# Second attention's stages begin with unit 4 of the second experts, and its values are divided by the softmax sums

## What is computed

```python
h = (x - mu) / jnp.sqrt(var + LN_EPS) * norm_w + norm_b
q, k, v = split(h @ qkv_w.T + qkv_b)                 # each L x C
w = jax.nn.softmax(jnp.einsum('ncq,nck->nqk', q, k * scale), axis=2)   # C x C
a = jnp.einsum('nqk,nck->ncq', w, v)
s = a @ proj_w.T + proj_b + x
# experts: every token is put in a slot of its two experts, 40 slots for each expert and row
y = relu(buf @ W1 + b1) @ W2 + b2;  f = sum over the two picks of p * y[slot]
x = x + s * silu(f)
```

## Time and profile before

| | |
|---|---|
| time, median of 3 runs | 1442.65 us (1442.06 to 1442.7) |
| profiled execution, its time | 1442.93 us |
| its span in the profile | 1441.2 us |
| busy: PE, DVE, ACT, POOL | 93%, 70%, 61%, 59% of the span |
| granted TensorE clock, mean | 0.988 of full speed |

### The profile page before, as it was taken

One profiled execution on the slowest core, in us unless ns is written; L12 is line 12 of the kernel. 1 busy time (PEld: TensorE's weight loads), 2 busy tenths in 40 slices (PEclk: granted clock), 3 DMA queues, 4 the chain that ended last, 5 costly groups with the idle time before them and its releaser, 6 DMA issues.

```text
span 1441.2 us, 32467 instructions
## 1 busy us (share of the span) xinstructions
PE 1344.9 (93%) x10039; PEld 1187.9 (82%) x10039; DVE 1007.4 (70%) x3163; ACT 879.5 (61%) x2257; POOL 845.3 (59%) x1675
## 2 busy tenths in 40 slices
PE   5999998998999999999999999999999999899964
PEld 4548897887899899899889988998998899788842
DVE  7817774666778677677768767776877777545765
ACT  3546775445677677677667667776767777522321
POOL 6257884443776665756656575565557576633462
PEclk9999999999999999999999999999999999999997
DMA  7017002423300000000000000000000000012231
GB/s 256 8 59 240 24 25 83 126 82 93 108 20 4 18 16 9 18 12 9 9 14 17 8 18 13 9 7 16 16 9 11 20 11 5 20 51 77 62 86 40
DMA packets 70203, 62.26 MB, mean 43 GB/s; under 512 B 10904, under 2 KB 58115, under 8 KB 70034
## 3 DMA queue, kind: packets, MB, share of 16 engines
q1 hardware_dynamic: 61842, 44.96, 10.3%
q0 software_dynamic: 8192, 15.23, 3.7%
HBM read 32.88 MB, written 25.17 MB: 40 GB/s over the span
## 4 chain that ended last, share of the span: by engine, by line
PE 79%; DVE 8%; issue 5%; POOL 4%; ACT 2%; DMA 1%; DVEq 1%; POOLq 0%; SPq 0%
PE sa L1895 17%; PE sc L1873 15%; PE mb L1902 13%; PE tr L1884 9%; PE sc L1732 4%; PE sc L1832 3%; PE mb L2113 2%; PE sc L1875 2%; DVE kept L1413 2%; PE sa L1737 1%; PE tr L1737 1%; POOL attn L799 1%; PE sc L2101 1%; POOL x_slots L770 1%; PE sc L1854 1%
## 5 line engine op out<-in xcount | busy, mean ns | idle before, releaser
L799 POOL TENSOR_SCALAR attn<-kept,rden 128x128 f32<-128x128 f32 (+3 forms) x512 | 289.4, 565 | 324.2 <-DVE rden L1417 299.1
L1406 DVE MAX8 top<-sc 128x8 f32<-128x144 f32 (+3 forms) x512 | 263.2, 514 | 221.4 <-PE sc L1875 219.4
L1873 PE MATMUL sc<-k_hl,x_hl 128*128 128x272 f32 (+3 forms) x1920 | 371.4, 313 | 3.2 <-DVE k_hl L1398 1.7
L1895 PE MATMUL sa<-wv,attnT 128*128 128x128 f32 x2560 | 370.8, 276 | 0.0
L1032 ACT ACTIVATE attnT<-tr 128x128 f32<-128x128 f32 (+3 forms) x512 | 223.2, 436 | 227.0 <-PE tr L1884 225.1
L1895 PEld LDWEIGHTS sa<-wv,attnT 128*128 128x128 f32 x2560 | 326.3, 192 | 2.0 <-issue 1.8
L1873 PEld LDWEIGHTS sc<-k_hl,x_hl 128*128 128x128 f32 x1920 | 282.0, 190 | 23.2 <-issue 13.0
L1026 ACT ACTIVATE ex<-sc,nmax 128x144 f32<-128x144 f32 (+3 forms) x512 | 276.9, 541 | 16.7
L1413 DVE SCALAR_TENSOR_TENSOR kept<-sc,top,ex 128x144 f32<-128x144 f32 (+3 forms) x512 | 284.3, 555 | 2.5 <-ACT ex L1026 0.8
L1884 PE MATMUL tr<-ident,attn 128*128 128x128 f32 x1280 | 229.5, 277 | 25.5 <-POOL attn L799 23.6
L1884 PEld LDWEIGHTS tr<-ident,attn 128*128 128x128 f32 x1280 | 138.9, 142 | 35.8 <-POOL attn L799 31.4
(11 more groups left out here) (334 smaller groups left out, 1935.8 us busy)
## 6 DMA issues: line engine op xcount, KB each, us to landing
x_slots<-sg SPq DMA_DIRECT2D x1, 4608.0 KB, 17.1
y_slots<-wv SPq DMA_DIRECT2D x18, 256.0 KB, 2.3
x_slots<-sg SPq DMA_DIRECT2D x1, 2560.0 KB, 16.5
y_pick<-x_slots SPq DMA_DIRECT2D x10, 256.0 KB, 2.8
fb<-L_ffn_b SPq DMA_DIRECT2D x2, 1024.0 KB
attn<-x_slots SPq DMA_DIRECT2D x8, 256.0 KB, 3.3
arena<-L_attn_x SPq DMA_DIRECT2D x8, 256.0 KB, 3.3
fb<-L_ffn_W SPq DMA_DIRECT2D x8, 256.0 KB, 6.3
```

Source lines behind the costliest of these rows:

```text
L799: pool.tensor_scalar(dst, src[:, NM:NM + P * (t + 1)], rden[:, t:t + 1], 1.0, ALU.mult, ALU.mult).then_inc(attn_ready.sem, 1)
L1406: dve.max(top8[:, t, :], src).then_inc(top_done.sem, 1)
L1873: pe.matmul(dst[:, lo:hi], x_hl[:, a, t * P:(t + 1) * P], k_hl[:, m, k, lo:hi], start=(i == 0), stop=(i == 2 and hi < w), skip_group_check ...
L1895: ins = pe.matmul(sa[:, t * C:(t + 1) * C], src[:, j * P:(j + 1) * P], wv[:, j, k, :], start=False, stop=False, skip_group_check=True)
```

## The change

The constant `C_FROM` = 4 takes the place of `E1` = 8: four slots go with each unit from unit 4 on, so slots 0 to 47 lie in units 4 to 15 and slots 48 to 69 in the tail. The slots behind which `take_z` and `gate` stand are renumbered. Units, slots and their matmuls are the same in number and shape. The second part: `weights` no longer multiplies the 128x128 weights by the reciprocal sums; ACT does it in the copy of the applied values (L1188), by a scale per partition, and PE turns the weights as soon as the exponentials are there. PE waits once more, at unit 4, for a read of bank `sa` (`sa_read`), and each `hnorm(r)` waits for its own row's kept input.

```diff
-        TAKE_Z = {16: 0, 24: 1, 32: 2, 36: 3, 44: 4, 52: 5, 60: 6, SLOTS_C: 7}
-        GATES = {18: 0, 26: 1, 34: 2, 38: 3, 46: 4, 54: 5, 62: 6, SLOTS_C + 1: 7}
+        TAKE_Z = {34: 0, 40: 1, 46: 2, 50: 3, 56: 4, 62: 5, 67: 6, SLOTS_C: 7}
+        GATES = {36: 0, 42: 1, 48: 2, 52: 3, 58: 4, 64: 5, 69: 6, SLOTS_C + 1: 7}
+        C_FROM = 4
...
                 if name == "apply":
                     act.wait_ge(aT_ps.sem, r + 1)
-                    act.activation(aT[r % 2], c_bank(i), ACT.Copy).then_inc(aT_ready.sem, 1)
+                    act.wait_ge(csum_ready.sem, r + 1)
+                    act.activation(aT[r % 2], c_bank(i), ACT.Copy, scale=csum[:, r % 2:r % 2 + 1]).then_inc(aT_ready.sem, 1)
...
             for n in range(UNITS_E):
-                slot = 4 * (n - E1)
+                slot = 4 * (n - C_FROM)
...
-                if n >= E1:
+                if n >= C_FROM:
                     evacuate_c(slot)
...
-            for i in range(4 * E1, SLOTS_C):
+            for i in range(4 * (UNITS_E - C_FROM), SLOTS_C):
                 evacuate_c(i)
...
             def hnorm(r):
                 dve.wait_ge(rstd1_ready.sem, rstd1_ready.at(r, 1))
+                dve.wait_ge(xn1_kept.sem, xn1_kept.at(r, 16))
...
-                dve.reciprocal(csum[:, r % 2:r % 2 + 1], csum[:, r % 2:r % 2 + 1])
-                dve.drain()
-                dve.tensor_scalar(cw[:, r % 2, :], cw[:, r % 2, :], csum[:, r % 2:r % 2 + 1], None, ALU.mult
-                                  ).then_inc(cw_ready.sem, 1)
+                dve.reciprocal(csum[:, r % 2:r % 2 + 1], csum[:, r % 2:r % 2 + 1]).then_inc(csum_ready.sem, 1)
...
-                if n == E1 - 1:
-                    dve.wait_ge(xn1_kept.sem, xn1_kept.at(B, 0))
+                if n == C_FROM - 1:
                     hnorm(0)
...
                 if name == "cwT":
-                    pe.wait_ge(cw_ready.sem, r + 1)
+                    pe.wait_ge(cexp_done.sem, r + 1)
...
+                if n == C_FROM:
+                    pe.wait_ge(sa_read.sem, sa_read.at(B - 1, 1))
```

More of the change, by code:

```diff
@@ L413, in build @@
         cexp_done = sig0("cexp_done")
-        cw_ready = sig0("cw_ready")
+        csum_ready = sig0("csum_ready")
         cwT_ps = sig0("cwT_ps")
```

## The result

The changed kernel takes **1438.33 us**, median of 11 runs (1437.14 to 1441.98); the kernel before took 1442.7 us beside it (11 runs, 1441.32 to 1444.17). The ratio is 0.997, with a 95% interval of 0.9961 to 0.9979. A second set of 5 runs took 1436.55 us, ratio 0.9957 (0.9944 to 0.9971). So it is faster by 0.2 to 0.6%, and the predicted 1438.7 us lies inside the first set of runs and 2.15 above the median of the second.

A forecast was written before the change was run, and what follows sets the result against it. The tail's serial slot chain bounds the kernel before, the gathers the changed one. Of 27.7 us off the tail, 10.8 come back in units and 12.9 go to gathers: 4.0 gained, 1442.65 to 1438.7 us, range 1435.3 to 1441.7.

The forecast's parts named there:

- Parts 1, 4 and 5: Units: two rows in, unit 14 10.27 us later; tail: slots wait on gathers, DVE free 5.7 us; end: span 4.0 shorter.
- the wait for block 8: At unit 8: PE's wait for the block's load goes, taking 1.33 us off the added cost of two rows.
- Part 2: Before unit 15's last relu: `take_z(2)` delays `down(15, 0)` and the gathers by 0.57 us, bounds 0 and 1.3.
- Part 3: POOL's 32 gathers of rows 4 to 7: first at 1385.83, 41.31 us to last start, row 7's data at 1429.7.
- the floor of 38.75: POOL's gathers of rows 4 to 7: 31 steps at 1.25 us throughout, in place of 41.31.
- Part 6: Sums divided later: only 0.3 us gained ahead of the gathers; about 1 us for each last row if gathers didn't bind.
- Gathers stretch: Rival, POOL's gathers: many more at the slow pitch, 0.50 us each, up to 12.9 more, 1451.6 us; chance 0.07.
- Units cost more: Rival, units 4 to 15: slots cost 0.25 us more a unit, 3 us lost, 1441.7 us; chance 0.08.
- Much faster: Rival, the end: gathers don't bind, the slot chain ends the kernel 16.8 us earlier, 1425.8 us; chance 0.03.

The follow-up runs named there:

- half_gathers: The changed kernel with 4 in place of 8 gathers for each of rows 4 to 7; 1424.15 us, ratio 0.9877.
- take2_late: The changed kernel with `take_z(2)` and gate 2 moved behind unit 15, from in front of its last relu; 1438.69 us, ratio 0.997.
- units_only: The changed kernel with weights still scaled by DVE and `cwT` waiting for them, so only the slots moved; 1437.29 us, ratio 0.9965.
- light_gates: The changed kernel with the gates of rows 3 to 6 replaced by one operation on one column; 1436.63 us, ratio 0.9961.
- after_again: The changed kernel measured once more with no edit; 1436.55 us, ratio 0.9957.
- sums_only: The kernel before (slots from unit 8) with only the later division by the sums, on values instead of weights; 1440.14 us, ratio 0.9985.
- from7: The changed kernel with slots beginning at unit 7 instead of 4, `take_z` and gates renumbered to suit; 1434.15 us, ratio 0.9944.

## Why the prediction was right, point by point

| step of the prediction | forecast | measured |
|---|---|---|
| unit 14 after unit 4 | 81.77 | 1362.42 - 1280.62 = 81.80 |
| unit 14 to `down(15, 0)` | 16.65 + 0.57 = 17.22 | 17.12 |
| first gather of row 4 after unit 4 | 105.51 | 105.51 |
| 32 gathers, first to last start | 41.31 | 40.29 |
| last gather to its data | 2.6 | 2.70 |
| DVE's wait for row 7 | 5.7 | 5.57 |
| row 7's `take_z` to the end | 7.45 | 7.48 |
| from unit 4 to the end | 156.88 | 155.98 |

**Parts 1, 4 and 5, the path and its new bound, were right.** Two rows cost what rows cost in units, the wait for block 8 went, and the end moved from the slots to the gathers. That the gathers bind is shown by half_gathers, and the 10.8 us that come back in the units by the first gather, 10.84 later than before from unit 4 on. The slots' chain runs at the gathers' pace as forecast: `take_z(4)`, `(5)` and `(6)` start at 1397.79, 1408.27 and 1418.44, each behind a wait for its gathers, where about 1398, 1408 and 1418.9 were given.

**Part 2, `take_z(2)`, was right in its sum and in its two terms.** The forecast was about 0.87 for the `take_z` and 0.3 back from the scaling, net 0.57. From unit 14 to `down(15, 0)` it took 16.65 us before, 17.12 in the changed kernel, 16.26 in take2_late (1376.92 - 1360.66) and 17.49 in units_only (1378.64 - 1361.15): 0.86 for the `take_z`, 0.37 back from the scaling, and 0.47 net. At the first gather the two are 0.93 and 0.38.

**Part 3, the gathers, is the term that was mis-sized:** 41.31 where 40.29 was measured. I had carried the slow gathers over one for one, since four gates lie under the gathers in both. In these profiles it is not the number of gates that goes with the time but which gather starts just behind the start of a two-input operation. With all of them in place the 32 gathers took from 40.29 to 41.74 us in ten profiles, and light_gates 39.24, near the floor of 38.75 of the prediction. This 1.02 us is all of the difference from unit 4 on but for 0.13 behind the last gather: 156.88 - 1.02 + 0.10 + 0.03 = 155.99.

**How near the total came is in part luck.** From unit 4 on the kernel was 0.90 us better than forecast, and unit 4 itself started 0.30 later, as the clock's fall and the stretch ahead of it happened to lie; other profiles have it up to 1.8 earlier. The median of 1438.33 is 0.37 below the forecast, that of after_again 2.15.

**Part 6, the sums, was right for this kernel** in that it is worth 0.38 us ahead of the gathers; what else it brings, 0.50, lies in the gathers' pace, which the forecast didn't see. ACT's copy takes the scale for 0.07 to 0.09 us, within the 0 to 0.1 given, to be set beside the earlier trace rows:

```profile
1389.17 0.67 ACT L1190 ACTIVATE attnT<-sc,csum 128x512 f32<-128x512 f32 x1
1402.55 0.69 ACT L1190 ACTIVATE attnT<-sc,csum 128x512 f32<-128x512 f32 x1 [1.78 <-PE sc L2149]
```

Its conditional, 1 us for each of the last three rows where the gathers don't bind, did not come in the profile where the slots end the kernel: in sums_only the three rows took 40.36 in place of 40.47. What it took for granted is that a wait taken out of a chain shortens it by its length; here the waits were shorter by that much and the granted clock was lower. It is not refuted either, as half_gathers ended 2.7 us earlier than the slots alone would without it.

**The rivals.** "Gathers stretch" did not come; its cause exists, but in few gathers. "Units cost more" is refuted by the 16.56 of each pair. "Much faster" is refuted by DVE's 5.57 us of waiting.

What stays open: what sets where in 1246 to 1266 us the clock falls, and so the scatter of unit 4's start; and whether the lower clock of sums_only's tail comes of the shorter waits or of scatter, since one profile shows the two together and others do not.

## What to carry to other kernels

Before serial work is moved under busy units, ask what waits for the end of those units: 27.7 us of slots left the tail here by the prediction's sum, 10.8 came back as a later start of the gathers, and the gathers then left 4 to 5. The best amount to move lies where the two chains meet, and the last wait says on which side a kernel is: if it ends with the gathers, move less; if it ends with the slots, move more. Here they meet between units 6 and 7, which end within 1.08 us of each other. Where one queue is the bound at its own pace, as the gathers are here, a change elsewhere was worth what it did to that queue's start and to the collisions on its way.

## What the hardware showed that I had not expected

The granted clock of a chain of hand-overs is not a fixed price. Three rows of sums_only's tail with 0.9 us less waiting each had a granted clock of 0.80, 0.83 and 0.76 instead of 0.88, 0.88 and 0.77, and 2.4 us more of PE's busy time for the same matmuls. But two profiles of one kernel had 0.89 and 0.79 in the same row, and from7 had 1.00 in a row that took 9.88 us and ends with a wait of 2.46 ahead of `cwT`. So one profile of such a stretch does not price a wait of under 1 us. Four matmuls of `sa<-qkvT,n_all` took 1.03 to 1.10 us at the upper of the clock's levels (2.4 GHz) and 1.98 to 2.05 at the lower one (1.2 GHz). Of the six falls of the clock in these three rows of before and of sums_only, five begin within 1.2 us of a `cwT`, during or just behind PE's wait of 3.1 to 4.0 us for it; the sixth, in sums_only, begins 1.7 us behind.

An indirect gather is as short as 0.94 us or as long as 1.59 on POOL, for the same form. The 1.59 is of from7, at 1393.18; the nearest operation with two inputs in SBUF (L1620) starts at 1393.27, behind it and not ahead, so that one is not explained by who was first. Two arrangements of DVE's work that differ by the place of one `take_z` and its gate (the change and take2_late) differ by 1.00 us over 32 gathers.
